# Edge walks of four graph attention layers: the chain from logits to exponents spread over two chunks, four slots of gathered rows, and gathers that wait for one weighing

## What is computed

```python
h = jnp.einsum('nf,fhd->nhd', x, W)                 # 8 heads of 32
a_src, a_dst = sum(h * att_src), sum(h * att_dst)   # per node and head
e = leaky_relu(a_src[src] + a_dst[dst], 0.2)        # logit of an edge
e_max = segment_max(e, dst); e_exp = exp(e - e_max[dst])
denom = segment_sum(e_exp, dst)
out = segment_sum(h[src] * (e_exp / denom[dst])[..., None], dst)
```

## Time and profile before

| | |
|---|---|
| median of three runs | 7074.7 us |
| profiled execution, whole | 7060.18 us |
| its span, first to last instruction | 7058.4 us |
| walk of stage 0 (names `l_edges`), first to last gather | 126.3 to 823.7 us |
| walk of stage 1 (`l_edges` again) | 1489.4 to 2168.0 us |
| first walk of stage 2 (`l2a_edges`) | 2534.1 to 3223.2 us |
| second walk of stage 2 (`l2b_edges`) | 3355.2 to 4041.8 us |
| mean granted clock of PE | 0.815 of full |

### The profile page before, as it was taken

One profiled execution on the slowest core, in us unless ns is written; L12 is line 12 of the kernel. 1 busy time (PEld: TensorE's weight loads), 2 busy tenths in 40 slices (PEclk: granted clock), 3 DMA queues, 4 the chain that ended last, 5 costly groups with the idle time before them and its releaser, 6 DMA issues. The chain is left out here.

```text
span 7058.4 us, 80551 instructions
## 1 busy us (share of the span) xinstructions
PE 4868.9 (69%) x19231; PEld 3367.9 (48%) x19232; DVE 3968.4 (56%) x8601; ACT 2368.3 (34%) x5719; POOL 2984.7 (42%) x2932
## 2 busy tenths in 40 slices
PE   2676749547775947775577747888898555377999
PEld 2444426325543734444344434444577333265666
DVE  3555633446667246665466656667324788686333
ACT  1333312123333224433243424455221222174333
POOL 2555432445552045552655526666000777352000
PEclk8778859768787968888688868889999666697999
DMA  4454414234442034443444411111001999673000
GB/s 116 137 163 153 114 54 126 90 102 141 141 144 62 1 108 144 136 143 87 141 136 144 130 42 27 30 30 27 22 7 52 362 368 377 213 228 98 9 13 23
DMA packets 543458, 819.10 MB, mean 116 GB/s; under 512 B 87966, under 2 KB 421967, under 8 KB 542839
## 3 DMA queue, kind: packets, MB, share of 16 engines
q1 hardware_dynamic: 396388, 432.93, 19.0%
q0 software_dynamic: 140832, 376.78, 18.9%
q10 hardware_dynamic: 5907, 5.92, 0.3%
HBM read 658.06 MB, written 157.71 MB: 116 GB/s over the span
## 5 line engine op out<-in xcount | busy, mean ns | idle before, releaser
L783 POOL DMA_INDIRECT l_edges_stage<-l_h_rows,src_t x832 | 802.1, 964 | 682.7 <-issue 217.9
L1096 PE MATMUL l_edges_ps_sum<-l_edges_msg,l_edges_hot 128*128 128x264 f32 x1664 | 595.1, 500 | 275.7 <-DVE l_attn_acc L925 179.8
L2492 POOL DMA_INDIRECT l_edge_kv<-l_kv_rows,src_t x416 | 476.3, 1145 | 673.2 <-POOLq L2400 516.8
L2918 POOL DMA_INDIRECT l_gate_edges_srow<-l_gate_src_rows,l_gate_edges_idx x512 | 487.2, 952 | 329.7 <-issue 142.3
L3054 PE MATMUL l_gate_edges_ps<-l_gate_edges_wide,l_gate_edges_hot_lo 128*128 128x500 f32 x1024 | 505.6, 636 | 102.5 <-issue 72.0
L1096 PEld LDWEIGHTS l_edges_ps_sum<-l_edges_msg,l_edges_hot 128*128 128x128 f32 x1664 | 354.1, 238 | 438.0 <-DVE l_attn_acc L925 257.7
L2545 PE MATMUL l_edge_ps_q<-l_q_q,l_edge_hot 128*128 x832 | 341.2, 581 | 303.9 <-issue 211.4
L783 POOL DMA_INDIRECT l2a_edges_stage<-l2a_h_rows,src_t x416 | 400.0, 961 | 340.8 <-issue 118.1
L783 POOL DMA_INDIRECT l2b_edges_stage<-l2b_h_rows,src_t x416 | 400.7, 963 | 329.0 <-issue 116.1
L2545 PEld LDWEIGHTS l_edge_ps_q<-l_q_q,l_edge_hot 128*128 128x128 f32 x832 | 231.8, 292 | 413.2 <-issue 367.4
L1096 PE MATMUL l2a_edges_ps_sum<-l2a_edges_msg,l2a_edges_hot 128*128 128x272 f32 x832 | 303.4, 508 | 159.6 <-DVE l2a_sums_acc L925 106.9
(11 more groups left out here) (786 smaller groups left out, 10893.5 us busy)
## 6 DMA issues: line engine op xcount, KB each, us to landing
l_edge_e<-e_rows SPq DMA_DIRECT2D x416, 128.0 KB
l_val_rows<-l_edge_vj SPq DMA_DIRECT2D x104, 512.0 KB
l_agg_stage<-l_val_rows SPq DMA_DIRECT2D x52, 1024.0 KB, 5.6
l_edges_rel_b<-rel_rows SPq DMA_DIRECT2D x52, 512.0 KB
l_edges_ea<-in_edge_attr SPq DMA_DIRECT2D x48, 512.0 KB
e_rows<-l_edges_e_s SPq DMA_DIRECT2D x48, 512.0 KB
l_experts_w<-in_L_ffn_w SPq DMA_DIRECT2D x32, 512.0 KB, 5.0
l_gate_edges_lo_b<-l_gate_edges_lo_rows SPq DMA_DIRECT2D x64, 256.0 KB
```

The lines of the kernel that those rows point to most:

```text
L783: nc.gpsimd.indirect_dma_start(out=stage[:, c % SL, u, :], out_offset=None, in_=h_rows, in_offset=bass.IndirectOffsetOnAxis(ap=K.src_t[:, ...
L1096: nc.tensor.matmul(ps_sum[u][:], hot[:, g, u, :], msg[:, g % 2, u, :], start=True, stop=True).then_inc(summed, 1)
L2492: nc.gpsimd.indirect_dma_start(out=kv[:, m, u, :], out_offset=None, in_=kv_rows, in_offset=bass.IndirectOffsetOnAxis(ap=K.src_t[:, n * EB ...
L2918: nc.gpsimd.indirect_dma_start(out=srow[:, n % 4, u, :], out_offset=None, in_=src_rows, in_offset=bass.IndirectOffsetOnAxis(ap=idx[:, n * ...
```

## The change

- DVE's chain is spread over two chunks. In chunk c it now does, in this order: weighing 0, rescaling, `tile_tops(c+1)`, `logits(c+2)`, weighing 1, `nodes_hot(c+3)`, adds of group 0, weighing 2, `tile_ends(c+2)` mixed with the adds of group 1, `edge_maxima(c+1)`, weighing 3, adds of group 2, `exponents(c+1)`, adds of group 3. PE's and ACT's instructions move to match; the turned logits get two places in PSUM.
- `stage` has 4 slots, and a gather for chunk c+4 waits for the weighing of chunk c alone.
- To make room, `rel_b` has one buffer in place of two, the side product is kept and stored in halves (two DMAs a chunk), and the zeros of the first walk are a quarter as wide and read four times by each DMA.
- DVE's loop holds 4 chunks, and 6 are written out behind it (before: 6, and 2).

```diff
-    SL, PER = 3, 6
+    SL, PER = 4, 4
+    REST = 2
...
             def _(pool):
                 for c in range(NCK):
                     for g in range(NG4):
                         if c >= SL:
                             pool.wait_ge(msg_built, NG4 * (c - SL) + g + 1)
-                            if g == 1:
-                                pool.wait_ge(lg_turned, c - SL + 2)
-                            elif g == 2:
-                                pool.wait_ge(ends_placed, c - SL + 2)
-                            elif g == 3:
-                                pool.wait_ge(inits_made, c - SL + 2)
...
                 def chunk(c, j, i, after):
                     weigh(c, i, 0)
                     blks = block_ids(nc, mybir.EngineType.DVE, K, c)
                     rescale(c, blks[0])
                     if after >= 1:
-                        logits(c + 1, j, i + 1)
-                    for g, step in enumerate((tile_ends, tile_tops, edge_maxima)):
-                        weigh(c, i, g + 1)
-                        if after >= 1:
-                            step(c + 1, i + 1, adds(c, g, blks))
-                        else:
-                            for u in range(GR):
-                                adds(c, g, blks)(u)
+                        tile_tops(c + 1, i + 1)
+                    if after >= 2:
+                        logits(c + 2, j, i + 2)
+                    weigh(c, i, 1)
+                    if after >= 3:
+                        nodes_hot(c + 3, j, i + 3)
+                    for u in range(GR):
+                        adds(c, 0, blks)(u)
+                    weigh(c, i, 2)
+                    if after >= 2:
+                        tile_ends(c + 2, i + 2, adds(c, 1, blks))
+                    else:
+                        for u in range(GR):
+                            adds(c, 1, blks)(u)
                     if after >= 1:
-                        exponents(c + 1, i + 1)
-                    if after >= 2:
-                        nodes_hot(c + 2, j, i + 2)
+                        edge_maxima(c + 1, i + 1)
+                    weigh(c, i, 3)
                     for u in range(GR):
-                        adds(c, GR - 1, blks)(u)
+                        adds(c, 2, blks)(u)
+                    if after >= 1:
+                        exponents(c + 1, i + 1, after >= 2)
+                    for u in range(GR):
+                        adds(c, 3, blks)(u)
```

And PE's chunk:

```diff
                 def chunk(c, m, after, j=None):
                     scatter(c, 0)
+                    if after >= 2:
+                        turn_logits(c + 2, m)
                     if after >= 1:
-                        turn_logits(c + 1, 1 - m)
+                        place_tops(c + 1)
                     if after >= 2:
                         turn_attr(c, m, 0, j * 16 + 16 * (m + 1))
                     scatter(c, 1)
-                    if after >= 1:
-                        place_ends(c + 1)
+                    if after >= 3:
+                        expand(c + 3, m, block_ids(nc, mybir.EngineType.PE, K, c + 3))
                     if after >= 2:
                         attr_terms(c, 0)
                     scatter(c, 2)
-                    if after >= 1:
-                        place_tops(c + 1)
                     if after >= 2:
                         turn_attr(c, m, 1, None)
-                    scatter(c, 3, 0, GR // 2)
                     if after >= 1:
+                        turn_maxima(c + 1)
                         place_f(c + 1)
-                        turn_maxima(c + 1)
-                    scatter(c, 3, GR // 2)
...
                     if after >= 2:
-                        blks = block_ids(nc, mybir.EngineType.PE, K, c + 2)
+                        place_ends(c + 2)
+                    scatter(c, 3)
                     if after >= 2:
                         attr_terms(c, 1)
-                        expand(c + 2, m, blks)
```

More of the change, by code:

```diff
@@ L859, in tile_ends, with tile_tops @@
                     add(3)
-                def tile_tops(c, i, add):
+                def tile_tops(c, i):
                     m = i % 2
@@ L874, in tile_tops, with edge_maxima @@
                                             ALU.mult).then_inc(tops_spread, 1)
-                    for u in range(1, GR):
-                        add(u)
-                def edge_maxima(c, i, add):
+                def edge_maxima(c, i):
                     cut_f, cut_r = (K.cuts[:, bass.ds(c, 1), a, :].rearrange("p c e -> p (c e)") for a in range(2))
@@ L956, in _ @@
                 logits(0, 0, 0)
-                for step in (tile_ends, tile_tops, edge_maxima):
-                    step(0, 0, lambda u: None)
                 nodes_hot(1, 0, 1)
-                exponents(0, 0)
-                with dve.Fori(0, (NCK - 2) // PER) as j:
-                    for i in range(PER):
-                        chunk(j * PER + i, j, i, 2)
-                chunk(NCK - 2, (NCK - 2) // PER, 0, 1)
-                chunk(NCK - 1, (NCK - 2) // PER, 1, 0)
+                tile_ends(0, 0, lambda u: None)
+                tile_tops(0, 0)
+                logits(1, 0, 1)
+                nodes_hot(2, 0, 2)
+                tile_ends(1, 1, lambda u: None)
+                edge_maxima(0, 0)
+                exponents(0, 0, True)
+                with dve.Fori(0, (NCK - REST) // PER - 1) as j:
+                    for i in range(PER):
+                        chunk(j * PER + i, j, i, 3)
+                LAST = (NCK - REST) // PER - 1
+                for i in range(PER + REST):
+                    c = LAST * PER + i
+                    chunk(c, LAST, i, min(3, NCK - 1 - c))
             @block.scalar
@@ L1134, in _ @@
                 turn_logits(0, 0)
+                expand(1, 1, block_ids(nc, mybir.EngineType.PE, K, 1))
                 place_ends(0)
+                turn_logits(1, 1)
                 place_tops(0)
+                expand(2, 0, block_ids(nc, mybir.EngineType.PE, K, 2))
+                turn_maxima(0)
                 place_f(0)
[L1138 to L1140 removed]
+                place_ends(1)
+                with pe.Fori(0, NCK // 2 - 2) as j:
                     for m in range(2):
[L1142 removed]
+                        chunk(j * 2 + m, m, 3, j)
+                LAST = NCK // 2 - 2
+                chunk(NCK - 4, 0, 3, LAST)
+                chunk(NCK - 3, 1, 2, LAST)
                 chunk(NCK - 2, 0, 1)
```

143 lines of the change are left out of this document (71 added, 72 removed).

## The result

The changed kernel took 7205.4 us, the median of four runs (7186.7 to 7222.2), beside 7069.8 (7063.2 to 7080.7) for the kernel before on the same chip: a ratio of 1.019, with a 95% interval of 1.0158 to 1.0221. It is slower, by 1.9%; forecast were 7200 us. Its profiled execution took 7196.6 us, 136.4 more than the one of before.

The account below looks back on a forecast made before the run. Taken as the bound: DVE waiting for PE results held while gathers run unbroken. Terms 12.6 + 15.1 + 4.4 - 6.3 + 6 = 31.8 us a walk, 127 for four; 7060 + 127 + 14, rounded 7200 us; range 6860 to 7340.

Parts of the forecast that it names:

- The reading of before: Walks of the kernel before: unbroken gathers hold PE's results until the stream runs dry; DVE stands still some 8 us a chunk.
- Step 1: DVE's chain in a chunk: the waits of 4.5 us before L866 and 1.4 before L899 go.
- Step 2: DVE's own work: uncovered gaps between adds and in short chains lengthen a chunk without gathers from 18.3 to 20.3 us.
- Step 3: Chunks 1 to 21: twelve-gather runs hold group 1's sums; period 27.2 us, middle of 25.6 and 28.8, against 26.6: +12.6 a walk.
- Step 4: Start of a walk: 64 gathers in front, not 52; first gather to second rescaling 110.1 us, not 95.0: +15.1.
- Step 5: DVE's loop turns: four a walk where there were three, +4.4 us a walk.
- Step 6: End of a walk: chunk 22 loses its gathers, -6.3 us; chunks 23 to 25 pay for DVE's new order, +6.
- A: Rival for the chunks with gathers: PE's results get through, period about 23.5 us, kernel 6890 us; chance 30%.
- B: Rival for the chunks with gathers: no contention, DVE is the bound near 21 us, kernel 6620 us; chance 7%.
- D: Rival for the chunks with gathers: more held, two adds or more and scatter 2; period 28.8 us, kernel 7335 us; chance 20%.

Follow-up runs that it names:

- Experiment 2: Kernel before with its gathers waiting for a weighing alone, three slots and old chain order kept: 7458.5 us, ratio 1.0543.
- experiment 9: Changed kernel with POOL also waiting, before a chunk's gather groups 1, 2 and 3, for PE's sums of the group before: 7073.2 us, ratio 1.0008.
- experiment 10: Changed kernel with only 8 gathers a chunk, not 16, from each walk's fifth chunk on (output not the reference's): 6686.4 us.
- Experiment 6: Changed kernel fetching 32 bytes a row, not 1056, after each walk's first four chunks, with as many gathers: 7170.8 us.
- Experiments 3 and 4: No gathers after each walk's first four chunks in the changed kernel, 6660.4 us, and after the first three in the kernel before, 6398.0 us.
- experiments 9 and 11: The second: changed kernel with the pauses of experiment 9 and DVE's loop of eight chunks run twice, ten written out: 6951.7 us, ratio 0.9913.
- experiment 1: Changed kernel whose third gather group of a chunk also waits for PE's four sums of group 1: 7169.3 us, ratio 1.0122.

## Why the prediction was right, by its steps

**The reading of before.** That long unbroken runs of gathers hold PE's results bore up best. Experiment 2 makes runs longer and loses 5.4% with nothing else changed; experiment 9 cuts them and wins back all of the change's loss; without gathers the waits of kind "remote" are gone. It doesn't hold for every run: experiment 10's runs of eight cost 0.3 us a chunk. One figure of the reading was off: DVE's standing still before was 27.2 - 16.7 = 10.5 us a chunk and not some 8, of which the three rows named make 7.5 and the turns 0.6; the sum didn't use it. The page "SBUF — State Buffer" of the Trainium skill, section "Who interferes with whom", says that DMA never contends with a compute engine. Taken as the prediction took it, as a rule for the time of the whole, the measurement decides against it here: without gathers the changed kernel takes 6660.4 us and not 7205.4, and the kernel before 6398.0 beside 7086.1. Experiment 6 agrees with it in so far as the bytes cost little. Whether anything contends inside SBUF, no run here shows.

**Step 1**, the chain off the path: right. L866's wait is 0.3 us in 21 chunks, and that of L895 (the L899 of before) 1.9.

**Step 2**, +2.0 us for the new order: not confirmed in size, and wrong in kind. Experiments 3 and 4 give 2.2, but at granted clocks of 0.89 and 0.97; at a clock of 1.00 one pair of chunks gives 0.9. I had it as gaps between DVE's own adds and in the short chains. The adds' idle time grew by 79.1 - 31.9 = 47.2 us in 21 chunks that grew by 45.9, and 47.3 of it is DVE waiting for PE's sums. That can be PE's slower products, or that the adds of a group now stand closer behind its weighing; the two weren't told apart.

**Step 3**, the period: right, and by the mechanism named. The third weighing ended 7.7 us after the rescaling (forecast 8.7), the last held result came at 17.7 (17.4), and the usual chunk took 25.8 to 28.0 us in `l2a` (27.2). One term of it was too long. In the chunk shown two adds and `edge_maxima` were left at 17.7, which by the prediction makes 28.8; it took 27.1, since the work behind came to 9.4 us and not 11.4. The middle of 25.6 and 28.8 was met with that luck. The 84 chunks with their turns cost 71 us more; steps 3 and 5 together said 4 x 17.0 = 68.

**Step 4**, the start: mis-sized, +24 us a walk and not +15.1. The stream is as forecast (80.5), but 7.8 + 21.9 behind it was the sum for a start in which chunk 0 was half done under the stream. Now 11.8 us pass to the first rescaling and a whole chunk of 26 to 31 follows, with new gathers that hold its results.

**Step 5**, loop turns: right as a sum, but the turn is not where its cost ends. Behind three turns of four in `l2a` the next chunk also took 31 us, in the one shown with sixteen gathers in a run.

**Step 6**, the end: mis-sized the other way, -8.7 us a walk and not -0.3. The chunks without gathers did not pay for the new order: 19.2 and 18.4 us, where 20.3 was forecast.

The errors of steps 4 and 6, +9 and -8 a walk, nearly cancel. So the 7200 was closer than its terms: right in direction, mechanism and period, with luck in the middle taken for step 3 and in steps 4 and 6, which cancel.

**The rivals.** Of A (the results get through) nothing was seen in the kernel as changed; that the order can gain once the runs are cut is true (26.6 and 25.5 us in experiments 9 and 11) but it stops well above A's 23.5. B is out. Of D two adds left at the stream's end were seen, but not its period: of the 52 chunks neither at a loop turn nor behind one, 2 took more than 28.8.

**What stays open.** Whether a product is late or only its signal; whether it is the issue of a gather or its 128 descriptors that matter; whether experiment 9 does better than experiment 1 only because it has no run of sixteen; why runs of eight cost nearly nothing in experiment 10; and what of the 2.2 us between experiments 3 and 4 is the clock's. A paced start together with the short pauses was not tried.

## What to carry to other kernels

A wait that looks superfluous may be pacing a stream: before taking it away, look at what the stream does when nothing holds it, and which results are due in that time. Where a producer has slack (POOL needed 20 of 27 us), let it wait for the consumer's late result rather than run ahead: in experiment 9 that won back all of the 1.9%. And work moved off one wait lands on the next; the sum of DVE's idle time, not the line that has gone, tells what a change is worth.

## What was unexpected of the hardware

- The effect is not linear in gathers: none, eight and sixteen a chunk gave 21.8, 22.1 and 28.1 us (means over 84 chunks).
- It hardly depends on bytes: 32 or 1056 a row, 208.1 or 215.5 us of waiting for the adds.
- The two kernels without gathers ran at granted clocks of 0.97 and 0.89 with the same products of PE in another order, and differed by 2.2 us a chunk; a comparison of two orders has to look at the clock first.
- A run of 64 gathers does not hold results to its end: DVE got one at 2660.30, 11.66 us after it began to wait and 4 us before the stream ended, and the next at 2673.77, after another 11.23 us of waiting and 9 us after the last issue.
- The same kernel before took 7008.3 and 7068.3 us on two occasions, 0.9% apart, so only ratios of kernels run side by side are compared here.
